# Separate PSUM bank pools for two kinds of matmul, with a shorter lead and shifted due times

## The reference

```
mod = (silu(c) @ wmod) -> sa, ca, ga, sb, cb, gb per batch      # ga, gb: sign kept, size at least 0.25
h = layernorm(x) * (1 + ca) + sa
x = x + ga * attention(h)        # 16 heads of 16; softmax(q k^T / 4) v; then proj_w, proj_b
h = layernorm(x) * (1 + cb) + sb
x = x + gb * ffn(h)
ffn(h): base = h @ W_base + b_base
        per batch, 8 autoencoders: relu(h @ W_enc + b_enc) @ W_dec + b_dec; the one with least mean squared error is chosen
        adapter_out = relu(h @ W_down[chosen] + b_down) @ W_up[chosen] + b_up
```

## Time and profile before

| | us |
|---|---|
| median of three runs | 984.89 |
| the profiled execution | 980.53 |
| its span, first to last instruction | 978.7 |
| TensorE busy | 945.7 |
| VectorE busy | 793.5 |
| ScalarE busy | 657.7 |
| GpSimd busy | 335.8 |

### The profile page before, as it was taken

The page is one execution under the profiler, slowest core; times in us unless marked ns, Lnnn a source line. Parts: engine busy times, 40 slices in busy tenths (PEclk is TensorE's granted clock), DMA queues, the critical chain, the costliest instruction groups (busy, mean ns, idle before and its releaser), DMA issues.

```text
span 978.7 us, 16476 instructions
## 1 busy us (share of the span) xinstructions
PE 945.7 (97%) x5794; PEld 475.7 (49%) x5794; DVE 793.5 (81%) x1629; ACT 657.7 (67%) x1295; POOL 335.8 (34%) x447
## 2 busy tenths in 40 slices
PE   6999999989999999999999999999999999999998
PEld 4444344434344355544454455445445465644486
DVE  4789988978888787887788888778878888888365
ACT  2148887877786777666668786766657867566930
POOL 4050234124364343111456543410165613116320
PEclk9889999999999899999999999999999999999999
DMA  6932061342525311416342411405434321132001
GB/s 180 144 73 39 23 110 46 61 93 73 94 49 89 60 36 35 77 27 110 99 105 50 87 35 46 75 14 88 127 82 83 52 36 36 39 98 79 30 6 49
DMA packets 47890, 66.93 MB, mean 68 GB/s; under 512 B 12139, under 2 KB 32112, under 8 KB 47796
## 3 DMA queue, kind: packets, MB, share of 16 engines
q1 hardware_dynamic: 46572, 65.00, 31.4%
q0 software_dynamic: 384, 0.79, 0.6%
q10 hardware_dynamic: 852, 0.09, 0.1%
HBM read 27.48 MB, written 12.59 MB: 41 GB/s over the span
## 4 chain that ended last, share of the span: by engine, by line
PE 75%; DVE 10%; DMA 5%; SPq 4%; ACT 2%; issue 2%; POOL 2%; ACTq 0%; DVEq 0%; POOLq 0%
PE pE L813 23%; PE pM L813 22%; PE pO L813 20%; PE pX L813 8%; DVE mx L1298 7%; SPq L1880 2%; DMA QO<-lo 1%; DMA xin<-in_x 1%; DMA QO<-mT 1%; ACT P L1120 1%; DMA outs<-osb 1%; PE pM L907 1%; ACT h1T L1161 1%; DVE junk L1435 1%; SPq L1938 1%
## 5 line engine op out<-in xcount | busy, mean ns | idle before, releaser
L1298 DVE TENSOR_REDUCE mx<-pE 128x1 f32<-128x512 f32 x440 | 287.2, 683 | 48.7 <-PE pE L813 47.4
L1298 DVE TENSOR_REDUCE mx<-pM 128x1 f32<-128x512 f32 x447 | 294.4, 683 | 31.2 <-PE pM L813 29.6
L1120 ACT ACTIVATE P<-pM 128x512 f32<-128x512 f32 x457 | 260.9, 602 | 69.2 <-PE pM L813 67.7
L1120 ACT ACTIVATE P<-pE 128x512 f32<-128x512 f32 x431 | 243.3, 602 | 86.9 <-PE pE L813 85.8
L813 PE MATMUL pO<-P,V 128*17 128x512 f32 x2048 | 261.7, 607 | 1.2 <-ACT osb L1127 1.0
L813 PE MATMUL pM<-KO,QO 48*128 48x512 f32 x447 | 178.7, 446 | 4.1 <-DMA QO<-lo 3.6
L813 PE MATMUL pM<-QO,KO 50*128 50x512 f32 x457 | 178.6, 435 | 1.0
L813 PE MATMUL pE<-KO,QO 48*128 48x512 f32 x440 | 175.0, 447 | 3.3 <-DVE mx L1298 2.5
L813 PE MATMUL pE<-QO,KO 50*128 50x512 f32 x431 | 166.2, 437 | 3.5 <-DMA QO<-mT 3.0
L813 PEld LDWEIGHTS pM<-QO,KO 50*128 50x128 f32 x457 | 80.8, 187 | 101.4 <-issue 70.8
L813 PEld LDWEIGHTS pE<-QO,KO 50*128 50x128 f32 x431 | 76.0, 187 | 99.4 <-issue 75.7
(11 more groups left out here) (303 smaller groups left out, 1323.0 us busy)
## 6 DMA issues: line engine op xcount, KB each, us to landing
outs<-osb SPq DMA_DIRECT2D x31, 256.0 KB, 2.2
KO<-hi SPq DMA_DIRECT2D x56, 128.0 KB, 4.0
QO<-hi SPq DMA_DIRECT2D x56, 128.0 KB, 5.6
x<-in_x SPq DMA_DIRECT2D x20, 256.0 KB, 3.5
out<-x SPq DMA_DIRECT2D x16, 256.0 KB, 2.1
AT<-outs SPq DMA_DIRECT2D x15, 256.0 KB
asum<-wsum SPq DMA_DIRECT2D x15, 256.0 KB
KO<-lo SPq DMA_DIRECT2D x28, 128.0 KB, 3.7
```

Source lines behind the costliest of these rows:

```text
L1120: e.activation(P[:, u % 3, j, :], bank(s), ACT.Exp).then_inc(*empties(s))
L1298: e.tensor_reduce(mx[:, hq % 2, k:k + 1, kh], bank(s), AX.X, ALU.max, negate=True).then_inc(*empties(s))
```

## The change

Six numbers of the planner change; `alone()` places up to three and one pieces of long steps instead of two and none; the banks are given in pools: M takes banks 0 to 2, E banks 3 to 5, another long step bank 6 if that was not yet used since the last burst, and otherwise the bank used longest ago out of 0 to 5 (or of all seven). After each enc eviction VectorE waits for the eviction's end and issues a no-op that counts up a new semaphore, s_Hf, and the `ehi` steps wait for that instead of the bank's count.

```diff
-SHARE = (1.3, 1.8, 1.8, 2.4)
+SHARE = (1.2, 1.8, 1.8, 2.4)
-LEAD = 50
+LEAD = 48
...
-        u = 200 if gi == 4 * NB - 1 else 16 * gi - 33
+        u = 200 if gi == 4 * NB - 1 else 16 * gi - 34
...
-                    u += (3, 2, 1, 0)[q]
+                    u += (2, 2, 1, 0)[q]
...
-            at(B + 5, ("pick", q), ("select", q), ("fetch", q))
+            at(B + 6, ("pick", q), ("select", q), ("fetch", q))
...
-                at(B + 14, ("ln1load", b + 1, k), ("ln1s", b + 1, k), ("ln1n", b + 1, k), ("ln1turn", b + 1, k))
+                at(B + 12, ("ln1load", b + 1, k), ("ln1s", b + 1, k), ("ln1n", b + 1, k), ("ln1turn", b + 1, k))
...
-                alone_long(u0 + 1, 2)
+                alone_long(u0 + 1, 3)
...
-                alone_long(u0, 0)
+                alone_long(u0, 1)
...
-            credit, filled = long(u, min(credit + SHARE[min(int(u) // UB, LAST)], 2 if light else 4.5), 2 - light)
+            credit, filled = long(u, min(credit + SHARE[min(int(u) // UB, LAST)], 2 if light else 3.5), 2 - light)
...
             elif s[0] == "E":
-                taken = {self.turn[x][0] for x in unfinished}
-                bank = min((x for x in range(7) if x not in taken), key=lambda x: at.get(x, -1))
+                bank = min(EB, key=lambda x: at.get(x, -1))
                 burst = n
             elif s[0] == "M":
 
-                taken = {self.turn[x][0] for x in unfinished}
-                bank = s[1] % 5 if s[1] < LEAD else min((x for x in range(7) if x not in taken), key=lambda x: at.get(x, -1))
+                bank = s[1] % 5 if s[1] < LEAD else min(MB, key=lambda x: at.get(x, -1))
                 burst = n
...
                 if begun and not late:
-                    free = (5, 6) if not kinds["E"] or kinds["M"] == NM else range(7)
+                    free = ((5, 6) if not kinds["E"] or kinds["M"] == NM else
+                            (XB,) if s[0] not in SHORT and at.get(XB, -1) < burst else
+                            MB + EB if unfinished or at.get(XB, -1) > burst else MB + EB + (XB,))
...
                     act.wait_ge(s_Hh, nth[s] - 1)
-                    act.wait_ge(*emptied("enc", b, t))
+                    act.wait_ge(s_Hf, nth["enc", b, t])
...
                     e.tensor_tensor(h2f[:, t % 2, :], bank(s), nbe[:, :], ALU.max).then_inc(*empties(s))
+                    dve.wait_ge(*emptied(*s))
+                    e.engine_nop().then_inc(s_Hf, 1)
...
-                    dve.wait_ge(*emptied("enc", b, t))
+                    dve.wait_ge(s_Hf, nth["enc", b, t])
```

More of the change, by code:

```diff
@@ L687, in adaln_block @@
         s_rsum, s_at = sem("rsum"), sem("at")
-        s_Hh, s_Hl, s_HL, s_Xh, s_Xl = (sem(n) for n in ("Hh", "Hl", "HLd", "Xh", "Xl"))
+        s_Hf, s_Hh, s_Hl, s_HL, s_Xh, s_Xl = (sem(n) for n in ("Hf", "Hh", "Hl", "HLd", "Xh", "Xl"))
         s_fill, s_rs1, s_xn, s_mhl, s_rs2, s_X = (sem(n) for n in ("fill", "rs1", "xn", "mhl", "rs2", "X"))
```

## The result

The changed kernel took 997.47 us (median of four runs, 996.72 to 1000.45) against 984.32 us, 13 us more. The recorded ratio is 1.0156, 95% interval [1.0136, 1.0177], which is 15 us (13 to 17); it lies above the 13, which fits the whole of the changed kernel's executions, 21 from 995.03 to 1001.06 with a median of 999.21. I had forecast 992.8 in a range of 981 to 1004. The profiled execution took 995.31 us (span 993.2, granted clock 0.990) beside 980.53 (978.7, 0.983) before.

The account below looks back on a forecast made before the run. TensorE's queue, busy 945.7 of 978.7 us and held mainly by PSUM banks VectorE had not drained, was taken as the bound; +6 + 1 - 1.1 + 2 + 0 + 0 = +7.9 on 984.9 gave 992.8 us, range 981 to 1004.

Parts of the forecast that it names:

- The banks: Bank pools for M and E: +6 us, a little over a quarter of the upper end of 21.6.
- The reading: Burst-by-burst check of each bank's release against the load three matmuls later: 80 bursts late, 79 after empty gaps, 21.6 us.
- rival (2): Bursts after gaps with two or more steps: pools uncouple E from VectorE, faster, 975 us; chance 0.15.
- against the upper end stands that other steps are relieved: Other steps, as the projection at 509.91 that waited 0.37 us for a reduction, would find bank 6 free.
- M loads' waits on reductions: Sign of a right forecast: the M part of the 38.3 us of weight-load waits on reductions more than doubles.
- E loads' waits on reductions: Sign of a right forecast: weight loads of E wait for reductions almost not at all, 17.2 us before.
- The reduction behind an enc: Sign of a right forecast: on VectorE the next reduction starts 0.05 us after the enc eviction.
- The stand at the sixth hand-over: TensorE's wait for handed-over maxima at 200.17, 2.68 us before, was to be near 4.5 us.
- The no-op: VectorE's extra wait behind 32 enc evictions, 0.13 us each: +1 us taken, bounds 0 and 4.2.
- The lead: Lead 48 instead of 50: -1.1 us at the first E, +2 for later hand-overs of maxima.
- Due times, share, cap, units without M: Moved steps and pieces: 0 us; -3 to +4 for due times, share and cap, -2 to +1 for units without M.
- Rival (1): Only the waiter changes, since reductions' rate and TensorE's own work set the pace: 986 us; chance 0.24.

Follow-up runs that it names:

- quick reductions: Each M reduction reads 256 of 512 columns: 955.94 us on the kernel before (ratio 0.9731), 968.39 us with the bank pools added (0.9855).

## Why the prediction was right, point by point

**The banks: sign and place of the first part right, size wrong.** I took +6 of a reading whose upper end was 21.6; the pools alone cost 17 us (1.0179 of 982, interval 13 to 22). The reading put 79 of its 80 late bursts after an empty gap. That part is real: +9.6 us in the pools alone, gone with quick reductions. I had discounted it by more than half as repaid. Only the stretches between bursts gave something back, 3 us in the pools alone (12.4 to 9.2), and nearly all of that is less time at half clock there; so next to nothing was repaid. What the reading could not see is the second part. It compared each E and M with the E or M three before it, as if nothing else used the pools. I even placed rival (2)'s gain in the bursts after two or more steps. There, in some 34 bursts, the pools alone cost +7.5 us, where the second step takes a bank of E's three. So the failed step is "against the upper end stands that other steps are relieved": the first long step is, at 509.91; the second and the short ones load E's pool, and the waits for their evictions before E loads rose by 27 to 29 us (4.8 before, 32.0 with the pools alone, 33.8 after). That price stands nowhere in the sum.

**What was to be seen.** M loads' waits on reductions more than doubled: 13.1 to 27.3 (26.7 and 0.6 in pE), as put. E loads' waits on reductions gone: as put, 17.2 to none named. The reduction behind an enc 0.05 us after it: 0.04. The stand at the sixth hand-over near 4.5 us: wrong. The timeline of SP's queue and TensorE after:

```profile
196.34 2.64 SPq L1940 DMA_DIRECT2D QO<-mT  x4
...
200.48 0.47 PE L813 MATMUL pE<-QO,KO 50*128 50x512 f32 x1 [0.77 <-DMA QO<-mT]
```

It is 0.77 us. The issue is 2.3 us later than in the earlier trace rows, but the E come only 4.1 us behind it instead of 6.1.

**The no-op**: +1 taken, 0 measured; the bounds (0 to 4.2) held. The 4.2 took one place for all 32; the 0.12 us are there behind 18. The Trainium skill's rule (VectorE: DVE Perf Modes, "The DRAIN you can't avoid") gave 0 for the sum, and the sum bears that out. Its reason fits only in part: the section says the next operation waits for the empty pipe anyway, but also that "A next op that is not held starts earlier". Here the start is 0.08 us before the eviction's end without the wait and 0.04 after it with it. That the kernel doesn't feel it because VectorE has slack there is my reading; no run tests it.

**The lead**: +1 taken (-1.1 and +2), -5.4 measured (982.03 to 976.60; by the ratio -3.3 to -6.5). The first E starts at 59.1 in the changed kernel instead of 60.2, as put, and at 59.6 with the lead alone. The +2 was wrong: by span times clock the lead gives -0.6, which can't be told from 0. Nearly all the rest is the granted clock, 0.987 instead of 0.982, for which the sum had no term. The kernel with everything but the pools shows the same rise, to 0.988.

**Due times, share, cap, units without M**: 0 taken. Everything but the pools is +0.1%, and the lead alone -0.5%, so the rest, with the no-op, costs about 5 to 6 us if the parts add. That is past my +4. By span times clock it is some 7 us (969.4 for everything but the pools, 962.3 before), hidden in the time by the higher clock. Nothing shows which number it is: seven numbers of the planner change, not the six that I counted, and only the lead was tried by itself. The units without M are part of the question: from E number 992 to 1023 the changed kernel loses 2.0 us.

**The sum** came out 5 us low by the medians of four (+7.9 for +13.2), 7 by the ratio. The bank term was 11 too small, the rest of the planner 5 to 6 too small, the lead 6 too dear. These errors partly cancel, and a clock that no term had in it gave back some 6 us in the profiled pair, so the hit owes much to luck. The parts do not simply add either: +17 for the pools and +1 for everything else make 18, and together they measured 13 to 15. Rival (1), only the waiter changes, fails on the last block: there the pools alone lose 7.0 us, and VectorE is not full (17.7 of 20 us at 840 before). In the first block, full on both engines, they lose 2.0 with the clock taken off, the least of the four, so in that place the rival had something. Rival (2) had its sign of decision right (E's waits down by 17, M's up by 14) and still lost, since the price was paid to the other steps.

## What to carry to other kernels

In this kernel one rotation over all banks was the best of the rules tried for a queue in order that writes a few PSUM banks. A bank kept for one kind of step is idle in every gap without that step, and here six banks instead of seven in turn cost 1.6 to 1.8%, whether the six were split or shared. When you read from a trace what a new rule would demand, put every user of the resource in, the rare ones too: the second step in a gap cost nearly as much as the 162 bursts that the reading was about. And before a gain of half a percent is put down to the schedule, multiply span by granted clock for every execution: the gain of the shorter lead, taken alone, vanishes in that product, while the cost of the pools stays (980.3 against 962.3).

## What the runs showed that I had not expected

Which of two pools needs the spare bank turns over with the speed of its reader: with 682 ns reductions a fourth bank is worth 12 us to M and 6 to E by the medians (14 and 9 by the ratios); with 418 ns reductions 1 and 11 (each together with the freer choice for the other steps). Shortening VectorE's work by 260 us (793.5 to 533.9) sped the kernel up by only 26; TensorE is 97% busy there too.
